# Attention scores: the relative position's terms from a matmul of their own, one copy of the key

## The reference

```python
q, k, v = qkv[0], qkv[1], qkv[2]            # (x @ w_qkv + b_qkv), heads split off
scores = jnp.einsum('bhqd,bhkd->bhqk', q, k) * scale
rel_pe = _relative_sinusoidal(t, hd, scores.dtype)   # sin and cos of (distance * frequency)
rel_bias = rel_pe @ w_rel                            # (2t-1, heads)
idx = jnp.arange(t)[:, None] - jnp.arange(t)[None, :] + (t - 1)
bias = jnp.transpose(rel_bias[idx], (2, 0, 1))[None]
attn = jax.nn.softmax(scores + bias, axis=-1)
out = jnp.einsum('bhqk,bhkd->bhqd', attn, v)
```

## Time and profile before

| | |
|---|---|
| median of 3 runs | 857.1 us (854.73, 857.1, 863.95) |
| the profiled execution | 861.1 us |
| its span in the profile | 859.3 us |
| attention's main loop, first to last scores | 241.2 to 651.8 us |
| PE, DVE, ACT busy from 400 to 440 us | 37.97, 36.53, 21.39 us |

### The profile page before, as it was taken

One profiled execution on the slowest core, in us unless ns is written; L12 is line 12 of the kernel. 1 busy time (PEld: TensorE's weight loads), 2 busy tenths in 40 slices (PEclk: granted clock), 3 DMA queues, 4 the chain that ended last, 5 costly groups with the idle time before them and its releaser, 6 DMA issues. The chain is left out here.

```text
span 859.3 us, 24631 instructions
## 1 busy us (share of the span) xinstructions
PE 690.2 (80%) x10030; PEld 527.5 (61%) x10030; DVE 599.7 (70%) x1199; ACT 349.9 (41%) x793; POOL 285.6 (33%) x361
## 2 busy tenths in 40 slices
PE   1769696461479999999999999999988479999960
PEld 1657543320257777777777777777766368888850
DVE  0627657843459899999899998998885246766525
ACT  1211111000035555555555555555454335555533
POOL 2474200002272333333233333332000455667333
PEclk9879899675779999999999999999998769999995
DMA  8990100005910000000000000000000412222117
GB/s 158 225 311 8 37 1 0 1 12 178 306 23 8 15 16 14 15 16 21 14 9 21 15 15 16 15 15 15 21 14 15 98 56 74 71 81 76 51 65 272
DMA packets 34786, 51.42 MB, mean 60 GB/s; under 512 B 9044, under 2 KB 26292, under 8 KB 34548
## 3 DMA queue, kind: packets, MB, share of 16 engines
q1 hardware_dynamic: 29524, 39.57, 16.2%
q0 software_dynamic: 5152, 10.29, 4.2%
HBM read 36.91 MB, written 18.00 MB: 64 GB/s over the span
## 5 line engine op out<-in xcount | busy, mean ns | idle before, releaser
L934 ACT ACTIVATE probT<-psP 82x328 f32<-82x328 f32 x256 | 112.1, 438 | 161.4 <-PE psP L834 161.4
L993 DVE TENSOR_REDUCE mx<-psS 82x8 f32<-82x656 f32 x128 | 106.5, 832 | 42.4 <-PE psS L825 42.2
L834 PE MATMUL psP<-ident_all,prob 82*82 82x82 f32 x1024 | 117.3, 236 | 22.5 <-ACT probT L934 22.4
L834 PEld LDWEIGHTS psP<-ident_all,prob 82*82 82x82 f32 x1024 | 89.8, 120 | 65.6 <-issue 25.9
L755 POOL TENSOR_TENSOR h_flat<-h_flat,po 128x256 f32<-128x256 f32 x41 | 29.7, 725 | 263.7 <-ACT po L921 263.7
L995 DVE TENSOR_TENSOR prob<-psS,mx 82x656 f32<-82x656 f32 x128 | 107.1, 837 | 4.4
L926 ACT ACTIVATE prob<-prob 82x656 f32<-82x656 f32 x128 | 94.8, 741 | 3.1 <-DVE prob L995 3.1
L802 PE MATMUL psQ<-hT,early 128*128 128x328 f32 x256 | 83.1, 449 | 0.6 <-ACT hT L903 0.5
L1005 DVE RECIPROCAL rden<-psO 128x164 f32<-128x164 f32 x64 | 74.8, 1169 | 4.4 <-PE psO L852 4.4
L812 PE MATMUL psQ<-early,hT 128*82 128x256 f32 x256 | 66.7, 383 | 0.1
L825 PE MATMUL psS<-kT,qT 32*82 32x82 f32 x2048 | 53.6, 242 | 0.0
(11 more groups left out here) (218 smaller groups left out, 1216.5 us busy)
## 6 DMA issues: line engine op xcount, KB each, us to landing
img<-in_x SPq DMA_DIRECT2D x6, 1008.0 KB, 19.5
out<-h_flat SPq DMA_DIRECT2D x41, 128.0 KB, 2.5
fused_rows<-in_txt SPq DMA_DIRECT2D x1, 4928.0 KB, 25.1
h_flat<-entry_rows SPq DMA_DIRECT2D x6, 512.0 KB, 6.5
h_flat<-fused_rows SPq DMA_DIRECT2D x1, 2176.0 KB, 16.2
ex_w2a<-in_ff_w_A SPq DMA_DIRECT2D x1, 2048.0 KB, 11.2
ex_w1b<-in_ff_w_B SPq DMA_DIRECT2D x2, 1024.0 KB, 16.7
out<-h_flat SPq DMA_DIRECT2D x8, 256.0 KB, 4.8
```

Source lines behind the costliest of these rows:

```text
L834: mm = te.transpose(psP[0:T, s * T:s * T + T], prob[:, b % 2, g, s, :], ident_all[0:T, 0:T])
L934: act.activation(probT[:, b % 2, g, :, :].rearrange("p s t -> p (s t)"), psP[0:T, 0:4 * T], ACT.Copy).then_inc(S["probT_ready"], 1)
L993: v.tensor_reduce(mx[:, half, :, :], s4, X, ALU.max).then_inc(S["max_ready"], 1)
```

## The change

- qT still has two copies of each query part, one for each head of a pair, with the other head's rows zero; they are now written by `tensor_scalar` (times ownq, plus bown). kT has one copy, unmasked, with its bias, written by ScalarE (read_k) and not by VectorE. In scores(b) the matmuls of both heads read the same kT.
- The tables stand alone: qrel [128, T], the same for all heads, and krel [128, 4, T], made from kt0, kt1 and wrel, one slice for each of the four heads of a partition group. scores(b) begins with one matmul for each g, qrel times krel, 328 columns wide, with start=True; the 16 matmuls of before then add to it with start=False.
- In the order of psQ's banks, parts j = 2, 3 now count with ACT's reads. read_k comes after exponent(b, 0) in turns with b % 4 >= 2, and read_q on DVE only in turns with b % 4 < 2. In the prologue ACT reads parts 2 and 3 ahead of copy_val(0).

```diff
-    by_act = {use: 1 + sum(u[0] != "qk" for u in uses[:k]) for k, use in enumerate(uses) if use[0] != "qk"}
-    by_dve = {use: 1 + sum(u[0] == "qk" for u in uses[:k]) for k, use in enumerate(uses) if use[0] == "qk"}
+    query = [use[0] == "qk" and use[1] % 4 < 2 for use in uses]
+    by_act = {use: 1 + query[:k].count(False) for k, use in enumerate(uses) if not query[k]}
+    by_dve = {use: 1 + query[:k].count(True) for k, use in enumerate(uses) if query[k]}
...
-                te.wait_ge(S["psQ_dve"], by_dve["qk", 4 * (b // 4) + 3])
+                te.wait_ge(S["psQ_dve"], by_dve["qk", 4 * (b // 4) + 1])
+                te.wait_ge(S["psQ_act"], by_act["qk", 4 * (b // 4) + 3])
+                if b == 0:
+                    te.wait_ge(S["krel_ready"], 1)
                 te.wait_ge(S["shifted"], 2 * b)
                 par, cols = b // 4 % 2, slice(T * (b % 4), T * (b % 4) + T)
+                for g in range(HG):
+                    rows = slice(32 * g, 32 * g + 32)
+                    te.matmul(psS[0:T, g, 0:4 * T], qrel[rows, :], krel[rows, :, :].rearrange("p s t -> p (s t)"), start=True, stop=False)
                 for t in range(2):
                     for a in range(2):
                         s = (2 * t + a) * T
                         for g in range(HG):
                             rows = slice(32 * g, 32 * g + 32)
-                            mm = te.matmul(psS[0:T, g, s:s + T], qT[rows, par, a, t, cols], kT[rows, par, a, t, cols],
-                                           start=True, stop=True)
+                            mm = te.matmul(psS[0:T, g, s:s + T], qT[rows, par, a, t, cols], kT[rows, par, t, cols],
+                                           start=False, stop=(t == 1 and a == 1))
                 mm.then_inc(S["scores_done"], 1)
...
+            def read_k(q, j):
+
+                act.wait_ge(S["qk_done"], 4 * q + j + 1)
+                if q >= 2:
+                    act.wait_ge(S["scores_done"], 4 * (q - 1))
+                act.activation(kT[:, q % 2, j - 2, :], bank(("qk", 4 * q + j))[:, 0:QT], ACT.Identity,
+                               bias=bqkv[:, j:j + 1]).then_inc(S["psQ_act"], 1)
...
             for n in range(3):
                 copy_xT(n)
+            read_k(0, 2)
+            read_k(0, 3)
...
                     exponent(b, 0)
+                if b // 4 + 1 < NQ and b % 4 >= 2:
+                    read_k(b // 4 + 1, b % 4)
...
-            def read_qk(q, j):
+            def read_q(q, j):
...
-                dst, scal, add, t = (qT, ownq, qadd, j) if j < 2 else (kT, own, kadd, j - 2)
                 for a in range(2):
-                    ins = v.scalar_tensor_tensor(out=dst[:, q % 2, a, t, :].rearrange("p (b t) -> p b t", b=4),
-                                                 in0=bank(("qk", 4 * q + j))[:, 0:QT].rearrange("p (b t) -> p b t", b=4),
-                                                 scalar=scal[:, a:a + 1], in1=add[:, a, t, :].unsqueeze(1).to_broadcast([128, 4, T]),
-                                                 op0=ALU.mult, op1=ALU.add)
+                    ins = v.tensor_scalar(qT[:, q % 2, a, j, :], bank(("qk", 4 * q + j))[:, 0:QT], ownq[:, a:a + 1], bown[:, a, j:j + 1],
+                                          ALU.mult, ALU.add)
...
-            for j in range(4):
-                read_qk(0, j)
+            for j in range(2):
+                read_q(0, j)
...
-                if b // 4 + 1 < NQ:
-                    read_qk(b // 4 + 1, b % 4)
+                if b // 4 + 1 < NQ and b % 4 < 2:
+                    read_q(b // 4 + 1, b % 4)
```

More of the change, by code:

```diff
@@ L680, in attention_block @@
         out_row = sb("out_row", [128, C])
-        qrel = sb("qrel", [128, 2, T]); kt0 = sb("kt0", [128, 2, T]); kt1 = sb("kt1", [128, 2, T])
-        wrel = sb("wrel", [128, 2, 2, 2]); own = sb("own", [128, 2]); ownq = sb("ownq", [128, 2])
+        qrel = sb("qrel", [128, T]); kt0 = sb("kt0", [128, T]); kt1 = sb("kt1", [128, T])
+        wrel = sb("wrel", [128, 4, 2]); own = sb("own", [128, 2]); ownq = sb("ownq", [128, 2])
         one2 = sb("one2", [T, 2, 32])
-        bown = sb("bown", [128, 2, 4])
-        qadd = sb("qadd", [128, 2, 2, T]); kadd = sb("kadd", [128, 2, 2, T])
+        bown = sb("bown", [128, 2, 2])
+        krel = sb("krel", [128, 4, T])
         mhalf = sb("mhalf2", [128, 1])
@@ L689, in attention_block @@
         hT = sb("hT", [128, 2, RH])
-        qT = sb("qT", [128, 2, 2, 2, QT]); kT = sb("kT", [128, 2, 2, 2, QT])
+        qT = sb("qT", [128, 2, 2, 2, QT]); kT = sb("kT", [128, 2, 2, QT])
         vv = sb("vv", [T, 4, 8, 2, 32])
@@ L782, in free @@
                     before = uses[k - 2]
-                    if before[0] == "qk":
+                    if before in by_dve:
                         te.wait_ge(S["psQ_dve"], by_dve[before])
@@ L1017, in _ @@
             for a in range(2):
-                v.tensor_scalar(bown[:, a, 0:2], bqkv[:, 0:2], ownq[:, a:a + 1], None, ALU.mult)
-                ins = v.tensor_scalar(bown[:, a, 2:4], bqkv[:, 2:4], own[:, a:a + 1], None, ALU.mult)
+                ins = v.tensor_scalar(bown[:, a, :], bqkv[:, 0:2], ownq[:, a:a + 1], None, ALU.mult)
             ins.then_inc(S["a_step"], 1)
[L1021 to L1025, removed]
+            for k in range(4):
+                ins = v.tensor_scalar(krel[:, k, :], kt0[:], wrel[:, k, 0:1], None, ALU.mult)
             ins.then_inc(S["a_step"], 1)
             v.wait_ge(S["a_step"], 3)
[L1028 to L1033, removed]
+            for k in range(4):
+                ins = v.scalar_tensor_tensor(out=krel[:, k, :], in0=kt1[:], scalar=wrel[:, k, 1:2], in1=krel[:, k, :],
+                                             op0=ALU.mult, op1=ALU.add)
+            ins.then_inc(S["krel_ready"], 1)
             v.wait_ge(S["out_row_ps"], 1)
             v.tensor_tensor(out_row[:], out_row[:], psO[:, 0:C], ALU.add).then_inc(S["out_row_ready"], 1)
-            for j in range(4):
-                read_qk(0, j)
+            for j in range(2):
+                read_q(0, j)
             early = [n for n in range(NTL) if turn_at[n] - 2 < 0]
@@ L1405, in shape_constants @@
     sin, cos = np.sin(pos * freq), np.cos(pos * freq)
-    qrel, kt0, kt1 = (np.zeros((128, 2, T), np.float32) for _ in range(3))
+    qrel, kt0, kt1 = (np.zeros((128, T), np.float32) for _ in range(3))
     own, one2 = np.zeros((128, 2), np.float32), np.zeros((T, 2, 32), np.float32)
@@ L1410, in shape_constants @@
         for g in range(HG):
[L1411 to L1415, removed]
+            own[32 * g + HD * a:32 * g + HD * a + HD, a] = 1.0
+    for g in range(HG):
+        lo = 32 * g
+        qrel[lo:lo + half], qrel[lo + half:lo + HD] = sin, cos
+        kt0[lo:lo + half], kt1[lo:lo + half] = cos, sin
+        kt0[lo + half:lo + HD], kt1[lo + half:lo + HD] = -sin, cos
     nn = NTOK // 128 * TOPK
@@ L1430, in relative_rows @@
     half = HD // 2
[L1431 to L1438, removed]
+    laid = np.zeros((128, 4, 2), np.float32)
+    for g in range(HG):
+        for k in range(2):
+            lo = 32 * g + half * k
+            for s in range(4):
+                for par in range(2):
+                    laid[lo:lo + half, s, par] = w_rel[par::2, 8 * (s // 2) + 2 * g + s % 2]
     return laid
```

## The result

The changed kernel takes 902.38 us (median of 4 runs, 900.51 to 902.69), the kernel before in the same session 855.91 (854.72 to 863.95). The ratio is 1.0517, with a 95% interval of 1.045 to 1.0584: 5% slower. The forecast was 886, slower, and the time lies at the very edge of its range, 902.38 against an upper end of 902. Sign and mechanism came out, the size less well: the loss is 46 us and not 29.

A forecast was written before the change was run, and what follows sets the result against it. Every block's loop, through PE, DVE or ACT, was taken to pass through the scores matmuls. Loop +31.9 us and prologue -2.5 gave +29.4; on the median of 857.1 that is 886.5, stated as 886, range 876 to 902.

The forecast's parts named there:

- The loop runs through the scores: Main loop: all block loops pass through the scores matmuls, so whatever is added there is added to each.
- r: Time the four new matmuls add to each of 64 blocks on PE: 0.57 us, bounds 0.50 and 2.29.
- Rival 2: New matmuls in scores: the four groups don't overlap when 328 wide; 941 us in pairs, 996 in a row; 4%.
- DVE's wait goes in blocks with project and a key part: ACT's chain comes next: 6.84 us without xT (+0.22, 10 blocks), 7.02 with xT (+0.40, 8 blocks).
- The query's read: DVE's two tensor_scalar from PSUM per query part: 0.95 us for the pair, where the old form took 1.01.
- The key's copy: ACT's 128x328 read from PSUM: about 0.44 us, mostly in an idle gap, moving the copies behind it by 0.06.
- rival 3: ACT's Identity read in the loop: needs its own table, two loads for each of 30 reads; +66, 952 us; 3%.
- rival 4: ACT's read_k costs its full length in the chain of copies, +0.34 more in 30 blocks: 897 us; 6%.
- The prologue and the clock: Ahead of the loop: -2.5 us without DVE's key reads; first blocks at a low clock level for another 1 us.
- The entries of the new matmuls cost nothing but their time on the array: PE in scores(b): eight entries priced as two steps of 0.286 us; the 16 matmuls that stay keep their price.
- The busy shares: In the loop: the vector engine's falls from 91% to about 78%, while PE's rises.
- Rival 1: New matmuls hide in PE's waits, r near 0, and DVE's shorter reads show: 849 us; sign turns below 0.12; 4%.

The follow-up runs named there:

- experiment 1: The changed kernel without the four new matmuls, so without the relative term: 857.67 us, kernel before 860.98, ratio 0.9975.
- experiment 2: The changed kernel with the four new matmuls issued twice: 934.37 us, ratio 1.0862 to the kernel before.
- experiment 3: The kernel before with four matmuls of 8 columns put ahead of each block's scores: 881.71 us, ratio 1.0243 to the kernel before.
- experiment 5: The changed kernel with the key's one copy made by VectorE, not ScalarE: 948.36 us beside 908.12 for the kernel before, ratio 1.0428.
- Experiment 4: The changed kernel with the 16 matmuls for the sums of probabilities merged to 8 of 164 columns: 895.74 us, ratio 1.0422 to the kernel before.

## Why the prediction was right, and where it was short

*The loop runs through the scores, so what they gain in length, every block gains.* Right: 0.55 in each block whose last link is the old one, and experiments 1 and 2 take away and add this alone. r was 0.57 in the sum; 0.55 measured. The 3.07 times of the Trainium skill (TensorE: Matmul & The Clock Gate, Measured speedup vs the span model), which would have made r 0.75, do not hold for these four matmuls: at 0.55 the eight entries run four at a time, as the old scores do. That r is streaming alone was too simple: 0.15 of it is there with 8 columns too (experiment 3). Rival 2 is out.

*DVE's wait goes in blocks with project and a key part, and ACT's chain is next.* Right: 6.89 and 7.07 against 6.84 and 7.02.

*The query's read, 0.95 for the pair.* Wrong: 1.13, 0.61 for an instruction, longer than the scalar_tensor_tensor (0.55) that I took as the upper end. The old form was no bound for an instruction with two operands from memory; with one, as in experiment 5, tensor_scalar takes 0.55. +0.16 in 18 blocks, 2.9 us.

*The key's copy, 0.44, in ACT's gap but for 0.06.* Mis-sized: 0.53, and 0.13. The nearest row was a Copy, the new one an Identity with a bias from memory. 2 us in all. Rivals 3 and 4 are out: the copy did not cost its full length, and no table load came into the loop.

*The prologue and the clock.* -2.5 forecast; the first scores come at 237.94, 3.3 earlier. The clock was not full through the whole loop in the kernel before either: until 247.1 us, in block 0, it was at the lower level. After the change its low slices fell otherwise: 253.0 to 256.5 us ran at the lower level (block 2, +1.6) and so did 683.1 to 686.5 (block 62, +1.1). The first is among what I had named, but I had put it at 1 us. Experiment 4 has the first again, none of the others has either, so I count them as chance of where the slices lie, without having shown it.

*The entries of the new matmuls cost nothing but their time on the array.* This is the step that failed: I counted their streaming and did not look at the length of PE's list. 5.9 us of stops in the loop follow from it; with narrow matmuls, which stream next to nothing, the stops were 10.4.

Together the loop came out 12 us longer than forecast: 5.9 of stops, 2.7 of clock, 2.9 of query reads, the rest of key copies, less what r and block 0 were set too high; on the profiled executions the loss is 41.4 and not 29.4. The other 5 us of the 17 by which the medians miss lie in the base: the profiled execution of before was one of its longer ones, 861.1 against a median of 855.91, while that of after, 902.55, was an ordinary one. That the time still lies at the edge of the range is luck: its upper end was set for rival 4 and a larger r, and neither came.

*The busy shares.* VectorE's in the loop fell from 89% to 75% (forecast: 91% to about 78%). That of PE, which I expected to rise, stayed: 93.9% before, 93.3% after.

*Rival 1, its turning point.* Borne out in kind: with r at nothing (experiment 1) the ratio is 0.9975; the forecast for it, 849, was too good, since it had the query's read 0.06 shorter and not 0.12 longer.

Open: what starts a fetch. The fetches followed by a stop start 0.9 to 2.1 us ahead of it, those in the kernel before some 5 to 6 us ahead of the border. Since nothing was tried that moves a fetch by itself, that a late fetch is the cause rests on these distances and on the number of entries.

## What to carry to other kernels

A bias folded into spare rows of a matmul was free on the matrix engine here (the scores take 0.83 us with it in the kernel before and without it in experiment 1); as a matmul of its own it cost 0.55 us in each turn, most of it for its columns, and when that matmul heads the loop through all engines nothing hides it. Relief for the second-busiest engine is worth only the wait it ends: VectorE was spared 28 us of work (599.7 to 572.1) and the kernel nothing (experiment 1). When entries are added to an unrolled list, compare its length for a turn with that of a fetched piece, see how soon after a fetch starts the list reaches the next border, and look for waits that the profile puts down to issue inside a group of matmuls.

## What the runs showed of the hardware

- PE's list is fetched in pieces of 16.4 KB, 256 entries (77, 81, 85, 89 fetches for lists that differ by 1024 entries or twice that), and PE can stop for 0.5 to 1.3 us at a border. It went on 2.2 to 2.8 us after the start of the last fetch in all 19 stops counted in two kernels.
- Four fp32 matmuls of 32 rows and 328 columns in four row groups and four banks: 0.55 us more in a block, two steps; with 8 columns 0.15; in bf16 0.18 to the next group, and 0.44 to 0.46 less in a block.
- VectorE's tensor_scalar from PSUM with two operands from memory, 128x328: 0.607 us, with one 0.549 (experiment 5); scalar_tensor_tensor of the same size 0.546. ScalarE's Identity, 128x328: 0.533 with a bias from memory, 0.62 with a scale too.
